# Selecting the top 256 tokens of each expert in token layout instead of in transposed layout

## The reference

```python
logits = xf @ Wr + br
Sm = softmax(logits, axis=-1)
G_t, idx_t = top_k(Sm.T, n_tok // E)
G, idx = G_t.T, idx_t.T
tokens = xf[idx]
Wu, bu = W_up[arange(E) // GS], b_up[arange(E) // GS]
mid = silu(einsum('keh,ehf->kef', tokens, Wu) + bu)
out = einsum('kef,efh->keh', mid, W_down) + b_down
y = zeros_like(xf).at[idx].add(G[..., None] * out)
x = x + 0.5 * y
```

## Time and profile before

| | |
|---|---|
| median of 3 runs | 1938.29 us (1937.61 to 1939.38) |
| the profiled execution | 1939.38 us |
| its span | 1937.1 us |
| TensorE busy | 1572.6 us, 81% |
| VectorE busy | 1299.3 us, 67% |
| ScalarE busy | 1013.1 us, 52% |
| GpSimd busy | 559.4 us, 29% |
| mean granted TensorE clock | 0.89 of full speed |

### The profile page before, as it was taken

The page is one execution under the profiler, slowest core; times in us unless marked ns, Lnnn a source line. Parts: engine busy times, 40 slices in busy tenths (PEclk is TensorE's granted clock), DMA queues, the critical chain, the costliest instruction groups (busy, mean ns, idle before and its releaser), DMA issues.

```text
span 1937.1 us, 25644 instructions
## 1 busy us (share of the span) xinstructions
PE 1572.6 (81%) x9076; PEld 1067.2 (55%) x9076; DVE 1299.3 (67%) x3062; ACT 1013.1 (52%) x1782; POOL 559.4 (29%) x527
## 2 busy tenths in 40 slices
PE   4997399999699699738998976986893499998694
PEld 3776033332477578517887965985881222224593
DVE  5687388894588734594434966596873488883884
ACT  2553167877455355225437722762661278884472
POOL 3674000000377200123016737663105000001403
PEclk9999579999799799878998987997995589998897
DMA  4110724300121200011000010002653723300473
GB/s 147 60 52 20 131 35 50 50 1 1 59 82 37 66 1 1 23 39 45 1 0 11 1 45 0 2 1 62 180 162 73 138 23 50 50 1 1 141 215 94
DMA packets 118633, 104.03 MB, mean 54 GB/s; under 512 B 20258, under 2 KB 104306, under 8 KB 118260
## 3 DMA queue, kind: packets, MB, share of 16 engines
q1 hardware_dynamic: 116458, 98.20, 21.6%
q0 software_dynamic: 2048, 4.20, 0.7%
HBM read 88.60 MB, written 13.76 MB: 53 GB/s over the span
## 4 chain that ended last, share of the span: by engine, by line
PE 48%; DVE 28%; POOL 9%; issue 5%; ACT 5%; DMA 3%; SPq 2%; POOLq 1%; DVEq 0%; ACTq 0%
PE bank L93 9%; PE bank L94 8%; PE bank L95 8%; PE bank L2261 5%; PE bank L2276 5%; DVE x L1469 4%; PE bank L2233 4%; DVE mx L2445 4%; DVE xn L213 2%; PE bank L2240 2%; POOL sorted_x L1956 2%; DVE q L685 1%; PE bank L185 1%; DVE st L195 1%; POOL yg L1961 1%
## 5 line engine op out<-in xcount | busy, mean ns | idle before, releaser
L2445 DVE TENSOR_REDUCE mx<-bank 128x1 f32<-128x512 f32 (+1 forms) x512 | 323.6, 680 | 74.0 <-PE bank L2233 71.3
L2377 ACT ACTIVATE e<-bank 128x512 f32<-128x512 f32 x512 | 276.7, 596 | 62.9 <-PE bank L2261 60.0
L2261 PE MATMUL bank<-qq,kk 99*128 99x512 bf16 (+1 forms) x512 | 160.8, 394 | 2.2 <-ACT e L2377 1.8
L2511 POOL TENSOR_TENSOR osb<-ot,rc 128x128 f32<-128x128 f32 x32 | 13.0, 407 | 500.8 <-DVE rc L2470 500.8
L1485 POOL TENSOR_TENSOR midl<-mid,midh 128x512 fp32r<-128x512 f32 (+1 forms) x96 | 132.2, 1383 | 77.5 <-ACT midh L1405 77.4
L1009 DVE TENSOR_TENSOR hl<-q,hh 128x512 fp32r<-128x512 f32 x64 | 47.6, 743 | 125.5 <-ACT hh L979 103.6
L185 PE MATMUL bank<-cf,xn 128*128 128x128 f32 x192 | 43.6, 369 | 105.8 <-DVE xn L213 93.5
L205 POOL TENSOR_SCALAR rs<-mv 128x4 f32<-128x4 f32 x52 | 13.0, 249 | 392.2 <-DVE mv L199 392.1
L93 PE MATMUL bank<-wdh,midh 128*128 128x256 f32 (+1 forms) x384 | 111.5, 290 | 10.8 <-DVE x L1469 10.5
L240 ACT COPY xT<-bank 128x512 f32<-128x512 f32 x44 | 25.8, 586 | 179.7 <-PE bank L185 179.4
L2361 ACT CAST qq<-bank 3x512 bf16<-3x512 f32 (+1 forms) x128 | 74.0, 578 | 80.7 <-PE bank L2240 77.5
(11 more groups left out here) (392 smaller groups left out, 4577.9 us busy)
## 6 DMA issues: line engine op xcount, KB each, us to landing
w<-in_L_ffn_W SPq DMA_DIRECT2D x30, 512.0 KB, 3.9
w<-in_L_ffn_W SPq DMA_DIRECT2D x30, 256.0 KB, 2.7
qq<-scratch SPq DMA_DIRECT2D x18, 384.0 KB
w<-in_L_ffn_w_kernel SPq DMA_DIRECT2D x16, 344.0 KB, 2.7
w<-in_L_ffn_w_kernel SPq DMA_DIRECT2D x16, 320.0 KB, 3.7
wo<-in_L_ffn_wo_kernel SPq DMA_DIRECT2D x16, 320.0 KB
scratch<-e SPq DMA_DIRECT2D x36, 128.0 KB, 2.4
w<-in_L_ffn_W SPq DMA_DIRECT2D x30, 128.0 KB, 3.6
```

The costliest lines, as they stand in the source:

```text
L2261: e.matmul(b_bank(t, u, j), keys(kk[0:K], t, b)[:, k * 128:(k + 1) * 128], queries(qq[0:K], t, b), start=True, stop=True).then_inc(*at_b.t ...
L2377: e.activation(er[u][:, j * 512:(j + 1) * 512], b_bank(t, u, j), ACT.Exp, bias=0.0, scale=scale).then_inc(*at_e.tick(n, t, u, j))
L2445: e.tensor_reduce(mxa[t % 3][:, o:o + nkb], bank[place_a["a", t, u, j]].rearrange("p (k n) -> p k n", k=nkb), X, ALU.max).then_inc(*at_max ...
```

## The change

The search is done in token layout: a partition holds a token of each tile, and all 8 experts of 16 tiles lie along it (128 values). The transpositions at both ends are gone. A step compares the 128 probabilities with 3 x 8 candidates in one instruction of 384 elements, with bf16 0/1 results (`cmpb`); a matmul with a matrix of ones sums over the 128 partitions, 384 columns wide; VectorE then reduces over the 16 tiles from PSUM (384 to 24), and chooses per expert. The ties are ranked by a matmul with a strictly triangular matrix and a scan over tiles, with seven small instructions behind it. TensorE's order begins with six `up` items, has no transpositions, and puts a count in when the sizes since the last are over 2.6. The ones of the high buffers are written by ScalarE behind the router's exponential, and GpSimd, which waits for that, writes the zeros of the low ones. In the constants, `same` and `earlier` (256 columns) make way for `coff` (128 columns), which no line reads.

```diff
@@ -1300,28 +1300,29 @@
             SAVED = 11
             wrb, bu, whu, whd, xs = pre.buf
             raw, tmp, gate = (te3(take(s, 128)) for s in ("raw", "tmp", "gate"))
-            mx, cnt, need = take("mx", 16), take("cnt", 4), take("need", 1)
-            rawT, gtT, eqT, pref = (take(s, 128) for s in ("rawT", "gtT", "eqT", "pref"))
-            junk = [take("junk", 128, BF16) for _ in range(3)]
+            mx, cnt, need = take("mx", 16), take("cnt", 24), take("need", 8)
+            cmpb = take("cmp", 384, BF16)
             mid = [take("mid", 3 * 512) for _ in range(2)]
             hl = [fine("mid", 3 * 512) for _ in range(3)]
             ysb = [take("ysb", 1024) for _ in range(SAVED)]
-            sel, cand = [take("sel", 4) for _ in range(2)], take("cand", 3)
+            sel = [take("sel", 32).rearrange("p (j e) -> p j e", e=8) for _ in range(2)]
+            cand = take("cand", 24).rearrange("p (j e) -> p j e", e=8)
+            tot, ahead = take("tot", 128), take("ahead", 128)
             nxt = prepare(m)
+            cmp_t = lambda o: cmpb[:, o:o + 128].rearrange("p (t e) -> p t e", e=8)
+            b8 = lambda z: z.unsqueeze(1).to_broadcast([128, NT, 8])
             bits = list(range(28, -1, -2))
             rows = lambda f: 128 if f < 2 else 85
             ups = [(i, f) for i in range(16) for f in range(3)]
             up_at = {u: k for k, u in enumerate(ups)}
 
-            order = [("up", 0, 0), ("turn", 0, 0), ("up", 0, 1), ("up", 0, 2), ("count", 0, 0), ("up", 1, 0), ("up", 1, 1), ("up", 1, 2)]
-            asked = [("count", s, 0) for s in range(1, 16)] + [("back", 0, 0)]
-            since = 9.0
+            order, counts, since = [("up", *u) for u in ups[0:6]], 0, 9.0
             for i in range(16):
                 for j in range(4):
                     for item, size in [(("down", i, j), 1.25)] + ([(("up", i + 2, j), 0.7)] if i + 2 < 16 and j < 3 else []):
-                        if since > 2.2 and asked:
-                            order.append(asked.pop(0))
-                            since = 0.0
+                        if since > 2.6 and counts < 16:
+                            order.append(("count", counts, 0))
+                            counts, since = counts + 1, 0.0
                         order.append(item)
                         since += size
                 order.append(("end", i, 0))
@@ -1330,21 +1331,13 @@
             def pe(q):
                 e = q.e
 
-                def turn_probabilities():
-                    q.wait_ge(*found.at(n, "raw"))
-                    transpose(e, bank[3][:, 0:128], raw.rearrange("p t e -> p (t e)")).then_inc(*counted.tick(n, "raw"))
-
-                def turn_gates():
-                    q.wait_ge(*gate_set.at(n))
-                    transpose(e, bank[3][:, 0:128], pref).then_inc(*counted.tick(n, "gates"))
-
                 def count(s):
                     q.wait_ge(*found.at(n, s))
                     if s < 15:
-                        a = e.matmul(bank[3][:, 0:3], cF("same"), cnt[:, 0:3], start=True, stop=True)
+                        a = e.matmul(bank[3][:, 0:384], onesb, cmpb[:, 0:384], start=True, stop=True)
                     else:
-                        e.matmul(bank[3][:, 0:1], cF("same"), cnt[:, 0:1], start=True, stop=False)
-                        a = e.matmul(bank[3][:, 0:1], cF("earlier"), cnt[:, 1:2], start=False, stop=True)
+                        e.matmul(bank[3][:, 0:256], onesb, cmpb[:, 0:256], start=True, stop=True)
+                        a = e.matmul(bank[3][:, 256:384], tri, cmpb[:, 128:256], start=True, stop=True)
                     a.then_inc(*counted.tick(n, s))
 
                 def up(i, f):
@@ -1374,10 +1367,6 @@
                 for s, i, k in order:
                     if s == "count":
                         count(i)
-                    elif s == "turn":
-                        turn_probabilities()
-                    elif s == "back":
-                        turn_gates()
                     elif s == "up":
                         up(i, k)
                     elif s == "down":
@@ -1390,6 +1379,8 @@
             def act(q):
                 e = q.e
                 router_act(q, n, tmp)
+                for h, l in hl:
+                    e.copy(h[64:128, 1024:1536], cF("onesrow")[64:128, :]).then_inc(*l2_m_hi.tick(n, "ones"))
 
                 def up(i, f):
                     fn, o = rows(f), slice(f * 512, (f + 1) * 512)
@@ -1400,7 +1391,7 @@
                     e.activation(z, bank[up_at[i, f] % 3][0:fn, :], ACT.Silu, bias=bu[0:fn, i % 4, f:f + 1]).then_inc(*gelu_set.tick(n, i, f))
                     if i >= 3:
                         q.wait_ge(*down_done.at(n, i - 3, 3))
-                    q.wait_ge(*w_lo.at(n, "ones"))
+                    q.wait_ge(*l2_m_hi.at(n, "ones"))
                     q.wait_ge(*gelu_set.now())
                     e.copy(hl[i % 3][0][0:fn, o], z).then_inc(*l2_m_hi.tick(n, i, f))
 
@@ -1430,32 +1421,36 @@
                 lg = te3(lg_sb[:, :])
                 chain(e.tensor_tensor(tmp, lg, wrb.unsqueeze(1).to_broadcast([128, NT, 8]), ALU.add))
                 router_dve(q, n, tmp, raw, tmp, mx)
-                e.memset(sel[0][:, 3:4], 0.0).then_inc(*found.tick(n, "raw"))
-                q.wait_ge(*counted.at(n, "raw"))
-                chain(e.tensor_copy(rawT, bank[3][:, 0:128]))
+                chain(e.memset(sel[0][:, 3, :], 0.0))
+                r4 = raw.unsqueeze(1).to_broadcast([128, 3, NT, 8])
                 for s, bit in enumerate(bits):
-                    now, lo = sel[s % 2], sel[s % 2][:, 3:4]
+                    now, lo = sel[s % 2], sel[s % 2][:, 3, :]
                     for j in range(3):
-                        a = e.tensor_scalar(cand[:, j:j + 1].bitcast(I32), lo.bitcast(I32), (j + 1) << bit, None, ALU.bitwise_or)
+                        a = e.tensor_scalar(cand[:, j, :].bitcast(I32), lo.bitcast(I32), (j + 1) << bit, None, ALU.bitwise_or)
                     chain(a)
-                    for j in range(3):
-                        a = e.tensor_scalar(junk[j], rawT, cand[:, j:j + 1], 0.0, ALU.is_ge, ALU.add, accum_out=cnt[:, j:j + 1])
-                    a.then_inc(*found.tick(n, s))
+                    e.tensor_tensor(cmpb.rearrange("p (j t e) -> p j t e", j=3, e=8), r4, cand.unsqueeze(2).to_broadcast([128, 3, NT, 8]),
+                                    ALU.is_ge).then_inc(*found.tick(n, s))
                     q.wait_ge(*counted.at(n, s))
-                    chain(e.scalar_tensor_tensor(now[:, 0:3], bank[3][:, 0:3], 256.0, cand, ALU.is_ge, ALU.mult))
-                    chain(e.tensor_reduce(sel[1 - s % 2][:, 3:4], now, X, ALU.max))
-                lo = sel[1][:, 3:4]
-                e.tensor_scalar(gtT, rawT, lo, 0.0, ALU.is_gt, ALU.add, accum_out=cnt[:, 0:1])
-                e.tensor_scalar(eqT, rawT, lo, 0.0, ALU.is_equal, ALU.add, accum_out=cnt[:, 1:2]).then_inc(*found.tick(n, 15))
-                q.wait_ge(*found.now())
-                e.tensor_tensor_scan(pref, cF("onesrow")[:, 0:128], eqT, 0.0, ALU.mult, ALU.add)
+                    chain(e.tensor_reduce(cnt.rearrange("p (j e) -> p j e", e=8),
+                                          bank[3][:, 0:384].rearrange("p (j t e) -> p j e t", j=3, e=8), X, ALU.add))
+                    chain(e.scalar_tensor_tensor(now[:, 0:3, :], cnt.rearrange("p (j e) -> p j e", e=8), 256.0, cand, ALU.is_ge, ALU.mult))
+                    chain(e.tensor_reduce(sel[1 - s % 2][:, 3, :], now.rearrange("p j e -> p e j"), X, ALU.max))
+                lo = sel[1][:, 3, :]
+                gt, eq = cmp_t(0), cmp_t(128)
+                e.tensor_tensor(gt, raw, b8(lo), ALU.is_gt)
+                e.tensor_tensor(eq, raw, b8(lo), ALU.is_equal).then_inc(*found.tick(n, 15))
                 q.wait_ge(*counted.at(n, 15))
-                chain(e.tensor_scalar(need, bank[3][:, 0:1], -1.0, 256.0, ALU.mult, ALU.add))
-                chain(e.scalar_tensor_tensor(eqT, pref, need, eqT, ALU.is_le, ALU.mult))
-                chain(e.tensor_tensor(gtT, gtT, eqT, ALU.add))
-                e.scalar_tensor_tensor(pref, gtT, 0.5, rawT, ALU.mult, ALU.mult).then_inc(*gate_set.tick(n))
-                q.wait_ge(*counted.at(n, "gates"))
-                chain(e.tensor_copy(gate, te3(bank[3][:, 0:128])))
+                et = lambda z: z.rearrange("p (e t) -> p e t", e=8)
+                chain(e.tensor_copy(et(tot), bank[3][:, 128:256].rearrange("p (t e) -> p e t", e=8)))
+                chain(e.tensor_reduce(cnt[:, 0:8], bank[3][:, 0:128].rearrange("p (t e) -> p e t", e=8), X, ALU.add))
+                e.tensor_scalar(need, cnt[:, 0:8], -1.0, 256.0, ALU.mult, ALU.add)
+                chain(e.tensor_tensor_scan(ahead, cF("scanreset"), tot, 0.0, ALU.mult, ALU.add))
+                chain(e.tensor_tensor(ahead, ahead, tot, ALU.subtract))
+                chain(e.tensor_tensor(tmp, te3(bank[3][:, 256:384]), ahead.rearrange("p (e t) -> p t e", e=8), ALU.add))
```

(17 more changed lines are left out.)

## The result

The changed kernel takes 1954.76 us in the median of six runs (1953.69 to 1960.95), the kernel before in the same series 1937.95 (1936.17 to 1939.38): ratio 1.0093, 95% interval 1.0079 to 1.0107, 16.8 us slower. The forecast was 1956, +17.6 on the profiled execution. The profiled execution after has a span of 1951.5 us (time 1953.5).

What follows compares the result with a forecast made beforehand. VectorE's chain of counts, gates and 88 adds was taken to set each stage's end. 5.6 us plus stalls of 2 x 6 gave +17.6 on 1939.4, 1957.0; the runs' median is 1.1 lower, so 1956, range 1943 to 1966.

Steps and rivals of the forecast that it cites:

- The stalls: TensorE's waits at the counts while GpSimd's lows hold VectorE up: 6 us a stage, bounds 0 and 11.
- The pattern: TensorE's stalls at the counts repeat after seven counts: 1.8, 0.55 and 0.5 us, and four counts without one.
- Small instructions: On VectorE, 3 or 4 elements cost 0.16 us and 256 cost 0.425, of which 0.16 doesn't depend on size.
- The tail: From count 15 to the first add: 5.0 us, +4.3 against before, with one wait for GpSimd of 1.3.
- The start: The first group of each stage ends about 1.0 us earlier in the first, 0 in the second.
- cheaper counts: On TensorE, fifteen counts cheaper by 0.035 us each give back 0.5 us.
- What lies behind the gates: VectorE's 88th add shifts with gates and TensorE's arrival: 2.3 us in the first stage, 3.3 in the second, plus stalls.
- 0.54 and 0.46: Weights at the 88th add: 0.54 of the gates' shift plus 0.46 of the shift in TensorE's arrival at `down(13, 0)`.
- Counts that keep up: Rival: VectorE's waits land in GpSimd's pauses, no stalls at the counts; +5.6 us or less, 1943 to 1944; chance 0.16.
- Short instructions: Rival: the Trainium skill's smaller fixed cost shortens VectorE's part of a count step by 0.5 us; 1949.5; chance 0.08.
- Faster: Rival: the later adds win the lock from GpSimd, TensorE doesn't wait at `down(13, 0)`; 1925.6 us; chance 0.06.
- no difference: Rival: a start 2 us better in both stages and no stalls at the counts; near 1940 us; chance 0.07.

## Why the prediction was right, step by step

*The stalls.* Forecast 6 us a stage, measured 5.3 and 6.3. The mechanism is shown by the candidates in PSUM, and from the other side by the instruction added to the kernel before. The pattern was wrong: not three stalls in seven repeated, but 2.55 or 3.33 at count 1, 1.5 at one more, 0.2 to 0.3 at five. I had laid out lows with pauses, while at the start they come in a row. And I had priced the candidates at 0.30 without a wait; in the form with one element they never waited (141 to 156 ns, though 72 of the 90 began during a low), with eight they do, up to 2.15 us. This agrees with the Trainium skill (SBUF — State Buffer, section on who interferes with whom): an SBUF to SBUF instruction of this kind can take the ports that VectorE shares with GpSimd, two SBUF inputs collide with a GpSimd instruction that reads SBUF, and a reduction never does (here 557 to 560 ns and 205 to 221 ns in 30 instances each). The step undisturbed was 2.4 us for 2.46.

*Small instructions.* The compare's shortest is 557 ns for my 0.56, the select's 182 for my 0.18. The rule of the Trainium skill (VectorE: DVE Perf Modes, the TRN2 errata), 58 cycles plus the elements, would have 460 and 85; the trace decides for the larger fixed part. The same section gives, as measured, (N + 151) / 0.96 ns for an fp32 tensor_tensor add of N elements: 557 and 182, as here. By my figures the short instructions save 0.4 us a step, not the 0.5 of the forecast, so that rival stood at about +13.

*The tail.* Forecast 5.0 us from count 15 to the first add, measured 6.17 in both stages. Three of its instructions waited, 2.6 us in all, not one for 1.3:

```profile
1080.38 0.91 DVE L1446 TENSOR_SCALAR need<-cnt 128x8 f32<-128x8 f32 x1
...
1082.38 1.01 DVE L1450 TENSOR_TENSOR tmp<-tmp,need 128x128 f32<-128x128 f32 x1
...
1083.76 1.40 DVE L1452 TENSOR_TENSOR tmp<-cmp,tmp 128x128 f32<-128x128 bf16 x1
```

L1446, eight elements SBUF to SBUF, is one of them; I had it at 0.16 and not exposed. (The rows add up to 1.9 us of exposed work where the forecast says 2.1.)

*The start.* Forecast -1.0 and 0. With the candidates in PSUM, where no count stalls, the arrival is 1.4 and 0.5 us earlier than before, for a forecast of 1.6 and 0.6 (start shift and cheaper counts). That is near, with some luck: the clock reaches 2.4 GHz 12.2 and 8.8 us after the stage's first matmul, in the kernel before after 10.8 and 8.0, which costs an estimated 0.7 and 0.4 us. The forecast has no such term; it names the clock only as a way to fail.

*What lies behind the gates* is the step that failed in size, though the sum hides it. The gates came 14.0 and 16.5 us later (forecast 11.6 and 12.6) and the arrival 5.3 and 8.3 (forecast 4.4 and 5.4). The longer tail (1.2 us), the stalls by the matmuls' starts (0.5 and 1.5 over the 6) and the clock (about 0.8 and 1.7) make up these differences in the gates to within 0.5 us. By 0.54 and 0.46 that makes 10.0 and 12.7 at the restart; measured are 7.5 and 10.1. The sum at the restart, 17.6, was hit by luck: late gates and a rule that weighed them too much cancelled. The wait at `down(13, 0)` was to be about 9 us and is 7.1 and 7.5. VectorE's adds of the second stage:

```profile
1277.05 16.90 DVE L1464 SCALAR_TENSOR_TENSOR x<-ysb,gate,x 128x128 f32<-128x128 f32 x32
...
1295.18 15.06 DVE L1464 SCALAR_TENSOR_TENSOR x<-ysb,gate,x 128x128 f32<-128x128 f32 x32
...
1312.38 6.36 DVE L1464 SCALAR_TENSOR_TENSOR x<-ysb,gate,x 128x128 f32<-128x128 f32 x24
...
1318.66 2.15 DVE L1464 SCALAR_TENSOR_TENSOR x<-bank,gate,x 128x128 f32<-128x128 f32 x8
```

The first 64 go at half speed as before (31.7 and 32.0 us in the two stages, before 33.0 and 32.8), the last 24 take 6.36 for 11.54 and 10.94 us. GpSimd stood before them, waiting for the statistics:

```profile
1312.56 0.24 POOL L205 TENSOR_SCALAR rs<-mv 128x4 f32<-128x4 f32 x1 [4.30 <-DVE mv L199]
1314.10 8.26 POOL L1481 TENSOR_TENSOR midl<-mid,midh 128x512 fp32r<-128x512 f32 x3
```

4.30 us of wait, then three lows shut out for 8.26 us by the adds. In the kernel before GpSimd has no such wait, and the adds and the lows take turns:

```profile
1293.29 10.94 DVE L1469 SCALAR_TENSOR_TENSOR x<-ysb,gate,x 128x128 f32<-128x128 f32 x24
```

```profile
1295.64 0.26 POOL L205 TENSOR_SCALAR rs<-mv 128x4 f32<-128x4 f32 x1
```

So gates that come late are partly paid back by a GpSimd that waits for them, which a constant rate can't show. The two kernels with that place moved show the sign in both directions; how much of the 2.5 us a stage it explains was not separated.

*The rivals.* Counts that keep up, 1943 to 1944: that is the kernel with candidates in PSUM (+4.6 us). Short instructions: their condition fails, since the shortest instances are those of the forecast. Faster, no difference: no sign of them.

*A better kernel.* Two small changes to the kernel before beat both: threshold 1.9 (0.9921, 0.9925) and the statistics at unit 10 (0.9926). They attack the same wait at `down(13, 0)`; both together were not run.

## What to carry to other kernels

When VectorE answers TensorE in a chain of small steps while GpSimd is busy, count each step's instructions that read two SBUF tiles or copy from SBUF to SBUF, and find GpSimd's rows without pauses: a 0.18 us instruction can cost 2.6. Moving one small operand to PSUM took all these waits in the steps away. A wait of TensorE too short for the list of matmuls can still be seen at its weight loads. An engine's wait for a late result can shield others from it, so before a late result is priced one for one, look at what stands still with it.

## What the runs showed of the hardware

A tensor-scalar instruction of eight int32 elements from SBUF to SBUF waits for GpSimd (157 ns shortest, 2154 longest), one of a single element does not (141 to 156 ns over 90 instances, 72 begun during a low). Against a row of lows without pauses VectorE's instruction waited for two of them (2.61 us), in one case for three (4.03 us for a compare of 0.56), and in the other direction 24 adds in a row held GpSimd's three lows for 8.2 us. A stall of 3.3 us in TensorE, with its clock at 2.4 GHz, was followed by a stretch at a mean of 0.76; stalls of 2.55 us in the changed kernel's first stage and of 3.0 us in the second with the fills on GpSimd were not.
